# Routed expert blocks in plain fp32: weights loaded straight to their place, sixteen splits off GpSimd, expert numbers read a block ahead

## The chip, the cores and the metric

The kernel runs on one core of a Trainium2 chip. The metric is the device time of one execution in microseconds. One core has a matrix engine (TensorE), a vector engine (VectorE), an activation engine (ScalarE), a general engine (GpSimd) and a queue engine (SyncE) that here only issues transfers. In the rows they are called PE (PEld is its weight load), DVE, ACT, POOL and SP.

## The reference

Four layers follow one another, each added to its input: an attention over 1601 context rows, a feed-forward with 16 experts, a second attention over the same context, and a second feed-forward. x is 4 x 256 rows of 256 numbers in fp32. Only the last layer is touched:

```python
def _L1_ffn_ref(x, router_w, router_bias, Wu, Wg, Wd, Su, Sg, Sd):   # DIM 256, EXPERT_DIM 128, 16 experts, top 2
    logits = flat @ router_w.T
    scores = jax.nn.softmax(logits, axis=-1)
    _, topk_idx = jax.lax.top_k(logits + router_bias, TOPK)
    topk_scores = jnp.take_along_axis(scores, topk_idx, axis=-1)
    topk_scores = topk_scores / topk_scores.sum(-1, keepdims=True)
    combine = jnp.einsum('nk,nke->ne', topk_scores, jax.nn.one_hot(topk_idx, N_EXPERTS, dtype=scores.dtype))
    for e in range(N_EXPERTS):
        h = jax.nn.silu(flat @ Wu[e]) * (flat @ Wg[e])
        out = out + combine[:, e:e + 1] * (h @ Wd[e])
    for s in range(N_SHARED):                                        # one shared expert, 256 wide
        out = out + jax.nn.silu(flat @ Su[s]) * (flat @ Sg[s]) @ Sd[s]
```

## The kernel before

The program is written out by hand, one stream of instructions for each engine with semaphores between them. It has four stages: A (first attention, and the keys and values of the second), B (first feed-forward), C (second attention, up to about 679 us) and D (second feed-forward).

Products need nearly fp32 precision. Mostly they are made of three fast ones: each operand is split into a rounded part (the _hi or h tiles, fp32r) and the rest (_lo or l), and the helper mm3 (L582, its three matmuls are L584 to L586) issues hi x hi, hi x lo and lo x hi into the same PSUM bank. In the second attention, the product of probabilities and values (L837) is a single plain fp32 matmul instead.

Stage D before the blocks. SyncE waits for the last attention output (cx_rdy), issues seven small loads of constants (L493: router weights, a triangle, block numbers and so on) and then loads 18 weight tiles of 128x768 through four staging buffers e_raw (expert_tile, L488), each reuse waiting for d_w. Two tiles belong to the shared expert, sixteen to the routed ones. A tile holds gate and up weights in its first 512 columns and down weights in the last 256. GpSimd splits each tile into e_hi (a cast, L566) and e_lo (a subtraction, L568). Meanwhile TensorE makes the output projection, VectorE adds the residual and normalizes in products of 128x256 (L1559, L1564), takes statistics again (L1179, L1182), normalizes for this layer (L1187), splits the router's weights (L1572, L1574), and with TensorE and ScalarE transposes the result (xTh, xTl). The router's matmuls follow, the top two experts are chosen on VectorE (L1591 to L1618), which ends in pos_i, the row number of each token in a list sorted by expert. Each expert's rows are padded to blocks of 128: 31 blocks (NBLK) in all. GpSimd then scatters the tokens into x_slots in memory (16 indirect transfers, L573), while TensorE does the shared expert.

The block loop. For block j, SyncE loads 128 rows (slots_in, L501, four buffers); TensorE transposes them (slots_T, L943); ScalarE writes xbh (L1156), VectorE xbl (L1657); TensorE reads the block's expert number into a register (value_load, L947) and makes gate and up in one 256 column product for each half of the input width, that is six matmuls by mm3 (gate_up); ScalarE applies silu (L1160), VectorE multiplies (L1661); TensorE transposes the hidden block (hidden_T, L962); ScalarE and VectorE split it (hbh L1164, hbl L1665); TensorE makes the down product, three matmuls (expert_down); VectorE copies it to yb (L1671), and SyncE stores it (L510). TensorE runs the stages of four blocks interleaved: transposes of j+2, gate and up of j+1, hidden transpose of j, down of j-1. After all blocks GpSimd gathers two rows per token (L579) and VectorE mixes them (L1687, L1689).

Ahead of stage B SyncE also fills x_slots with zeros (L430) and then goes on with B's weight tiles (load_rest, L329).

Of the kernel before, what the change touches and what calls it, by code (L numbers as in the profile page):

```python
# [71 lines left out]
def build(nc, a, out, stop="D"):  # L72
# [8 lines left out]
    with ExitStack() as ctx:  # L81
# [95 lines left out]
        with ExitStack() as s:  # L177
# [3 lines left out]
            e_hi = Dt("e_hi", [P, NTILE, WC], F32R)  # L181
# [5 lines left out]
            xbh, xbl = Dt("xbh", [P, 2, KT * P], F32R), Dt("xbl", [P, 2, KT * P], F32R)  # L187
            sb_, hb = Dt("sb_", [P, 2, P]), Dt("hb", [P, 2, P])
            hbh, hbl = Dt("hbh", [P, 2, P], F32R), Dt("hbl", [P, 2, P], F32R)
# [3 lines left out]
            Dt("gap2", [P, 560])  # L193
            e_lo = Dt("e_lo", [P, NTILE, WC], F32R)
            e_raw = Dt("e_raw", [P, 4, WC])
# [63 lines left out]
        d_in = [sem(f"d_in{n}") for n in range(4)]  # L259
# [3 lines left out]
        xT_rdy, xb_hi, xb_lo, GU_rdy, sl_rdy, hm_rdy, hT_rdy, hb_hi, hb_lo, Y_rdy, y_ev = (  # L263
            sem(n) for n in ("xT_rdy", "xb_hi", "xb_lo", "GU_rdy", "sl_rdy", "hm_rdy", "hT_rdy", "hb_hi", "hb_lo", "Y_rdy", "y_ev"))
# [56 lines left out]
        def _(sp):  # L321
# [100 lines left out]
            for t, s in ((wq_raw[:], a["wqT"].rearrange("(k p) n -> p k n", p=P)), (bq[:], a["bq"]),  # L422
                         (wo_raw[:], a["woT"].rearrange("(k p) n -> p k n", p=P)),
                         (bo[:], a["bo"].rearrange("(o n) -> o n", o=1).broadcast_to([P, D])),
                         (gam[:], a["gam"].rearrange("(o n) -> o n", o=1).broadcast_to([P, D])),
                         (bet[:], a["bet"].rearrange("(o n) -> o n", o=1).broadcast_to([P, D])),
                         (rs[:], a["rs"].rearrange("(o n) -> o n", o=1).broadcast_to([P, 1]))):
                sp.dma_start(t, s).then_inc(cw_in, 16)
            for h in range(2):
                sp.dma_start(xs_d.rearrange("(j p) d -> p j d", p=P)[:, :, h * P:(h + 1) * P], zero[:].bitcast(F32).unsqueeze(1).broadcast_to([P, NBLK, P])).then_inc(x_zero, 16)  # L430
# [54 lines left out]
            def expert_tile(k):  # L485
# [4 lines left out]
            for t, s in ((gw_raw_d[:], a["gw1"].rearrange("(k p) n -> p k n", p=P)), (gb_d[:], a["gb1"].rearrange("(o n) -> o n", o=1).broadcast_to([P, E])),  # L490
                         (rev[:], a["rev"]), (tri_d[:], a["tri16"]), (steps[:], a["steps"]), (blk[:], a["blk"]),
                         (up_raw[:], a["upper"])):
                sp.dma_start(t, s).then_inc(d_cst, 16)  # L493
            for k in range(NTILE):
                expert_tile(k)
# [22 lines left out]
        def _(pool):  # L518
# [45 lines left out]
            for k in range(NTILE):  # L564
# [24 lines left out]
        def _(pe):  # L589
# [300 lines left out]
            def shared_hidden(n):  # L890
                k, half = n // 2, n % 2
                ct = SC0 + n
                s = slice(half * 512, half * 512 + 512)
                pe.wait_ge(d_w, k + 1)
                pe.wait_ge(silu_rdy, ct)
                for q in range(KT):
                    w = slice(q * 2 * P, q * 2 * P + P)
                    mm = mm3(pe, ps[:, 4, :], e_hi[:, k, w], e_lo[:, k, w], xTh[:, q, s], xTl[:, q, s], q == 0, q == 1)
                mm.then_inc(G_rdy, 1)
                pe.wait_ge(mul1_rdy, ct)  # L900
                for q in range(KT):
                    w = slice(q * 2 * P + P, (q + 1) * 2 * P)
                    mm = mm3(pe, ps[:, 5, :], e_hi[:, k, w], e_lo[:, k, w], xTh[:, q, s], xTl[:, q, s], q == 0, q == 1)
                mm.then_inc(U_rdy, 1)

            def shared_down(n):
                k, half = n // 2, n % 2
                pe.wait_ge(hl_rdy, SC0 + n + 1)
                for j in range(4):
                    t, s = 4 * half + j, slice(j * P, (j + 1) * P)  # L910
                    mm = mm3(pe, ps[:, t // 2, (t % 2) * D:(t % 2 + 1) * D], hh_d[:, half, s], hl_d[:, half, s],
                             e_hi[:, k, 2 * D:3 * D], e_lo[:, k, 2 * D:3 * D], False, False)
# [25 lines left out]
            def slots_T(j):  # L938
                pe.wait_ge(xb_in[j % XR], 16 * (j // XR + 1))
                if j >= 2:  # L940
                    pe.wait_ge(xb_lo, j - 1)
# [3 lines left out]

            def gate_up(j):
                expert[j] = pe.value_load(eb_i[0:1, j:j + 1], min_val=0, max_val=E - 1)  # L947
                pe.wait_ge(xb_lo, j + 1)
                if j >= 2:
                    pe.wait_ge(hm_rdy, j - 1)  # L950
                for k in range(KT):
                    w = slice(k * 2 * P, (k + 1) * 2 * P)
                    rh, rl = (t[:, NSH1:NTILE, w][:, bass.ds(expert[j], 1), :].rearrange("p o n -> p (o n)") for t in (e_hi, e_lo))
                    s = slice(k * P, (k + 1) * P)
                    mm = mm3(pe, ps[:, 2 + j % 2, 0:2 * P], xbh[:, j % 2, s], xbl[:, j % 2, s], rh, rl, k == 0, k == 1)
                mm.then_inc(GU_rdy, 1)

            def hidden_T(j):
                pe.wait_ge(hm_rdy, j + 1)
                if j >= 2:  # L960
                    pe.wait_ge(hb_lo, j - 1)
                pe.transpose(ps[:, 4 + j % 2, 0:P], hb[:, j % 2, :], ident[:]).then_inc(hT_rdy, 1)  # L962

            def expert_down(j):
                pe.wait_ge(hb_lo, j + 1)
                if j >= 2:
                    pe.wait_ge(y_ev, j - 1)
                rh, rl = (t[:, NSH1:NTILE, 2 * D:3 * D][:, bass.ds(expert[j], 1), :].rearrange("p o n -> p (o n)") for t in (e_hi, e_lo))
# [17 lines left out]
        def _(act):  # L986
# [167 lines left out]
            def slots_hi(j):  # L1154
                act.wait_ge(xT_rdy, j + 1)
                act.activation(xbh[:, j % 2, :], ps[:, j % 2, 0:KT * P], ACT.Copy).then_inc(xb_hi, 1)  # L1156
# [5 lines left out]
            def hidden_hi(j):  # L1162
                act.wait_ge(hT_rdy, j + 1)
                act.activation(hbh[:, j % 2, :], ps[:, 4 + j % 2, 0:P], ACT.Copy).then_inc(hb_hi, 1)  # L1164

            for j in range(-2, NBLK + 1):
                if j + 2 < NBLK:
                    slots_hi(j + 2)
                if 0 <= j + 1 < NBLK:
                    gate_silu(j + 1)  # L1170
                if 0 <= j < NBLK:
                    hidden_hi(j)
# [3 lines left out]
        def _(dve):  # L1176
# [478 lines left out]
            def slots_lo(j):  # L1655
                dve.wait_ge(xb_hi, j + 1)
                dve.tensor_tensor(xbl[:, j % 2, :], ps[:, j % 2, 0:KT * P], xbh[:, j % 2, :].bitcast(F32), ALU.subtract).then_inc(xb_lo, 1)  # L1657

# [3 lines left out]

            def hidden_lo(j):
                dve.wait_ge(hb_hi, j + 1)
                dve.tensor_tensor(hbl[:, j % 2, :], ps[:, 4 + j % 2, 0:P], hbh[:, j % 2, :].bitcast(F32), ALU.subtract).then_inc(hb_lo, 1)  # L1665
# [7 lines left out]
            for j in range(-2, NBLK + 1):  # L1673
                if j + 2 < NBLK:
                    slots_lo(j + 2)
                if 0 <= j + 1 < NBLK:
                    hidden_mul(j + 1)
                if 0 <= j < NBLK:
                    hidden_lo(j)
# [69 lines left out]
```

## Time and profile before

| | us |
|---|---|
| three runs | 871.08, 874.21, 874.29 |
| median | 874.21 |
| the profiled execution | 871.58 |
| its span in the profile | 869.7 |
| stage D in it, from 679 | 190.7 |
| of that, the block loop from its first transpose to the start of its last copy to yb | 64.4 |

Times in the rows are microseconds from the start of the span; durations of one instruction are in ns where the row says mean. A matmul's record includes the time in which the array fills and drains, so that records of one engine overlap; the distance of two starts is what one costs. The share of busy time is that of an engine over the span.

### The profile page before, as it was taken

To read this page: it belongs to the slowest core of one execution; us is meant where nothing else is said; L and a number is where in the kernel's file an instruction comes from. 1 tells how busy PE (TensorE), PEld (TensorE's weight loads), DVE (VectorE), ACT (ScalarE), POOL (GpSimd) and SP (SyncE) were. 2 spreads that over 40 slices of the span, in tenths; PEclk is the share of its full clock that TensorE was granted. 3 is DMA by queue.
4 is the path that set the end of the run, shared out by engine and by line. 5 is a ranking of instruction groups with operands and counts; after the bars stand their busy time and mean duration, and the time that the engine had idled before them with its cause. 6 is when DMAs were issued, how large, how long until landed. Compare 5 with 4: busy or idle time off the path is not lost.

```text
span 869.7 us, 14654 instructions
## 1 busy us (share of the span) xinstructions
PE 710.4 (82%) x5556; PEld 537.7 (62%) x5556; DVE 571.9 (66%) x1077; ACT 395.7 (45%) x555; POOL 156.6 (18%) x126
## 2 busy tenths in 40 slices
PE   4899998996789999999956999999999504858850
PEld 3778787984678888888843444444444302647740
DVE  7765656555866666666664777777777796546633
ACT  2524242433122222223226999999999201234420
POOL 6343434200000000000000000000000498330015
PEclk9999999997999999999986999999999855969995
DMA  6474746429333334333792999968840442134424
GB/s 216 159 226 145 227 158 214 177 85 306 98 90 108 119 92 126 96 115 105 140 161 51 195 147 122 194 89 145 140 61 2 129 136 73 37 107 130 135 85 127
DMA packets 63977, 114.52 MB, mean 132 GB/s; under 512 B 12064, under 2 KB 42272, under 8 KB 62896
## 3 DMA queue, kind: packets, MB, share of 16 engines
q1 hardware_dynamic: 61376, 108.30, 49.4%
q0 software_dynamic: 1536, 4.20, 1.5%
q10 hardware_dynamic: 1008, 1.25, 0.4%
q8 instruction: 38, 0.62, 0.4%
q14 instruction: 19, 0.16, 0.1%
HBM read 78.86 MB, written 31.70 MB: 127 GB/s over the span
## 4 chain that ended last, share of the span: by engine, by line
PE 42%; issue 16%; ACT 16%; POOL 9%; DVE 8%; DMA 6%; SPq 2%; POOLq 0%; ACTq 0%; DVEq 0%
ACT p L1130 13%; PE ps L584 12%; PE ps L585 11%; PE ps L586 11%; POOL e_lo L568 3%; PE ps L837 2%; DMA raw<-in_ctxT 2%; PE ps L819 2%; DMA raw<-in_ctxN 2%; POOL yg L579 2%; POOL cTl L557 2%; POOL e_hi L566 1%; POOL cNl L544 1%; DMA k_lo<-kl 1%; ACT cNh L1029 1%
## 5 line engine op out<-in xcount | busy, mean ns | idle before, releaser
L1130 ACT ACTIVATE p<-ps,kbias 128x1024 f32<-128x1024 f32 (+1 forms) x208 | 208.6, 1425 | 1.3 <-PE ps L819 1.3
L1509 DVE TENSOR_SCALAR p<-p 128x1024 f32<-128x1024 f32 (+1 forms) x208 | 144.1, 693 | 58.0 <-ACT p L1130 56.5
L837 PE MATMUL ps<-p,vsl 128*17 128x256 f32 (+1 forms) x1664 | 113.3, 387 | 0.7 <-DVE p L1509 0.7
L819 PE MATMUL ps<-qst,kst 48*128 48x256 f32 (+1 forms) x832 | 100.0, 329 | 14.4 <-DMA qst<-ql 5.9
L819 PEld LDWEIGHTS ps<-qst,kst 48*128 48x128 f32 (+1 forms) x832 | 61.2, 186 | 75.7 <-ACT p L1130 45.0
L1092 ACT ACTIVATE hh<-h 128x512 fp32r<-128x512 f32 x50 | 31.6, 632 | 138.7 <-DVE h L1441 114.8
L562 POOL MEMSET ones<- 128x128 f32 x1 | 0.2, 206 | 508.2 <-DMA up_raw<-in_upper 508.2
L584 PE MATMUL ps<-xTh,w_hi 128*128 128x512 f32 x200 | 80.0, 400 | 5.2 <-DVE h L1437 4.4
L585 PE MATMUL ps<-xTl,w_hi 128*128 128x512 f32 x200 | 79.3, 397 | 0.0
L586 PE MATMUL ps<-xTh,w_lo 128*128 128x512 f32 x200 | 79.2, 396 | 0.0
L837 PEld LDWEIGHTS ps<-p,vsl 128*17 128x17 f32 (+1 forms) x1664 | 37.7, 97 | 37.6 <-issue 3.9
L584 PE MATMUL ps<-w_hi,hh 128*128 128x256 f32 x200 | 57.7, 289 | 1.5 <-DVE hl L1443 1.5
L1443 DVE TENSOR_TENSOR hl<-h,hh 128x512 fp32r<-128x512 f32 x50 | 34.6, 692 | 36.6 <-ACT hh L1092 36.6
L1437 DVE TENSOR_TENSOR h<-silu,ps 128x512 f32<-128x512 f32 x50 | 34.4, 688 | 36.5 <-PE ps L586 22.6
L585 PE MATMUL ps<-w_lo,hh 128*128 128x256 f32 x200 | 57.4, 287 | 0.0
L586 PE MATMUL ps<-w_hi,hl 128*128 128x256 f32 x200 | 57.2, 286 | 0.0
L595 PE MATMUL ps<-ident,xn 128*128 128x128 f32 x48 | 11.8, 426 | 51.2 <-DVE xn L1187 51.2
L584 PEld LDWEIGHTS ps<-xTh,w_hi 128*128 128x128 f32 x200 | 38.0, 190 | 13.4 <-DVE h L1437 5.8
L544 POOL TENSOR_TENSOR cNl<-raw,cNh 128x1024 fp32r<-128x1024 f32 (+1 forms) x16 | 31.3, 1980 | 78.7 <-ACT cNh L1029 78.7
L586 PEld LDWEIGHTS ps<-xTh,w_lo 128*128 128x128 f32 x200 | 37.9, 189 | 9.0
L595 PEld LDWEIGHTS ps<-ident,xn 128*128 128x128 f32 x48 | 9.4, 222 | 53.0 <-DVE xn L1187 53.0
L585 PEld LDWEIGHTS ps<-xTl,w_hi 128*128 128x128 f32 x200 | 37.9, 189 | 6.6
(279 smaller groups left out, 1653.6 us busy)
## 6 DMA issues: line engine op xcount, KB each, us to landing
kst<-k_hi SPq DMA_DIRECT2D x64, 200.2 KB, 7.6
w_raw<-in_w SPq DMA_DIRECT2D x25, 384.0 KB, 3.0
v_one<-vst SPq DMA_DIRECT2D x4, 1768.0 KB, 9.2
vsl<-v_one SPq DMA_DIRECT2D x4, 1768.0 KB, 15.7
e_raw<-in_w SPq DMA_DIRECT2D x18, 384.0 KB, 3.0
kst<-k_lo SPq DMA_DIRECT2D x32, 200.2 KB, 8.4
raw<-in_ctxN SPq DMA_DIRECT2D x12, 512.0 KB, 6.0
k_hi<-kh SPq DMA_DIRECT2D x24, 256.0 KB, 2.6
```

What stands on the lines that cost most here:

```text
L544: pool.tensor_tensor(cNl[:, c0:c0 + w, :], src, cNh[:, c0:c0 + w, :].bitcast(F32), ALU.subtract).then_inc(ctx_split, 1)
L568: pool.tensor_tensor(e_lo[:, k, :], e_raw[:, k % 4, :], e_hi[:, k, :].bitcast(F32), ALU.subtract).then_inc(d_w, 1)
L584: e.matmul(o, lh, rh, start=first, stop=False, skip_group_check=True)
L585: e.matmul(o, lh, rl, start=False, stop=False, skip_group_check=True)
L586: return e.matmul(o, ll, rh, start=False, stop=last, skip_group_check=True)
L819: mm = pe.matmul(ps[0:rows, 2 * (x % RING) + t, c * SEQ:(c + 1) * SEQ], kst[r, job % KSL, c, m * P:m * P + rows], qst[r, b, 2 * g + c, :], ...
L837: mm = pe.matmul(ps[32 * j:32 * j + VW, 6 + job % 2, 0:SEQ], vsl[0:rows, b % 2, at_:at_ + VW], p32[0:rows, x % PBUF, (2 * t + c) * SEQ:(2 ...
L1092: act.activation(hh[:, half, :], h32[:, half, :], ACT.Copy).then_inc(hh_rdy, 1)
L1130: act.activation(p32[0:rows, x % PBUF, :], psf[0:rows, bank * 512:bank * 512 + 1024], ACT.Exp, scale=0.25, bias=kbias[0:rows, col:col + 1] ...
L1437: dve.tensor_tensor(h32[:, half, :], silu[:, half, :], ps[:, 5, :], ALU.mult).then_inc(mul1_rdy, 1)
L1443: dve.tensor_tensor(hl[:, half, :], h32[:, half, :], hh[:, half, :].bitcast(F32), ALU.subtract).then_inc(hl_rdy, 1)
L1509: dve.tensor_scalar(t, t, CLO, CHI, ALU.max, ALU.min).then_inc(p_clip, 1)
```

## The change

Five things change, all in stage D:

- The constants' seven loads are issued ahead of the zero fill of x_slots, before stage B, not after the attention.
- All 18 weight tiles are loaded unsplit into one tile e_w: two transfers of a tile for the shared expert, two of eight tiles each for the routed ones. No staging buffers are left, so no load waits for GpSimd.
- GpSimd splits only the two shared tiles, into sh_hi and sh_lo.
- In the block loop the operands aren't split: ScalarE writes xbT and hbT as plain fp32, VectorE's two subtractions are gone, and each mm3 becomes one plain fp32 matmul.
- The expert number of block j+2 is read after gate and up of block j+1 (expert_of), not directly before its use.

```diff
@@ SyncE, ahead of stage B
+            for t, s in ((gw_raw_d[:], ...), (gb_d[:], ...), (rev[:], a["rev"]), (tri_d[:], a["tri16"]), (steps[:], a["steps"]), (blk[:], a["blk"]), (up_raw[:], a["upper"])):
+                sp.dma_start(t, s).then_inc(d_cst, 16)
             for h in range(2):
                 sp.dma_start(xs_d..., zero...).then_inc(x_zero, 16)
             load_rest(FFN["B"])
@@ SyncE, after the attention (the same seven loads are gone from here)
             sp.wait_ge(cx_rdy, NJ)
-                if k >= 4:
-                    sp.wait_ge(d_w, k - 3)
-                sp.dma_start(e_raw[:, k % 4, :], a["w1"][k]).then_inc(d_in[k % 4], 16)
+            for k in range(NSH1):
+                sp.dma_start(e_w[:, k, :], a["w1"][k]).then_inc(d_in[0], 16)
+            for n in range(2):
+                sp.dma_start(e_w[:, NSH1 + 8 * n:NSH1 + 8 * n + 8, :], a["w1"][...].rearrange("k p c -> p k c")).then_inc(d_in[1], 16)
@@ GpSimd
-            for k in range(NTILE):
-                pool.wait_ge(d_in[k % 4], 16 * (k // 4 + 1))
-                pool.tensor_copy(e_hi[:, k, :], e_raw[:, k % 4, :]).then_inc(d_hi, 1)
+            for k in range(NSH1):
+                pool.wait_ge(d_in[0], 16 * NSH1)
+                pool.tensor_copy(sh_hi[:, k, :], e_w[:, k, :]).then_inc(d_hi, 1)
                 pool.wait_ge(d_hi, k + 1)
-                pool.tensor_tensor(e_lo[:, k, :], e_raw[:, k % 4, :], e_hi[:, k, :].bitcast(F32), ALU.subtract).then_inc(d_w, 1)
+                pool.tensor_tensor(sh_lo[:, k, :], e_w[:, k, :], sh_hi[:, k, :].bitcast(F32), ALU.subtract).then_inc(d_w, 1)
@@ TensorE, block loop
             def gate_up(j):
-                expert[j] = pe.value_load(eb_i[0:1, j:j + 1], min_val=0, max_val=E - 1)
-                pe.wait_ge(xb_lo, j + 1)
+                pe.wait_ge(xb_ev, j + 1)
...
-                    mm = mm3(pe, ps[:, 2 + j % 2, 0:2 * P], xbh[:, j % 2, s], xbl[:, j % 2, s], rh, rl, k == 0, k == 1)
+                    mm = pe.matmul(ps[:, 2 + j % 2, 0:2 * P], xbT[:, j % 2, k * P:(k + 1) * P], weights_of(j, slice(k * 2 * P, (k + 1) * 2 * P)),
+                                   start=k == 0, stop=k == KT - 1, skip_group_check=True)
...
             def expert_down(j):
-                mm3(pe, ps[:, 6 + j % 2, 0:D], hbh[:, j % 2, :], hbl[:, j % 2, :], rh, rl, True, True).then_inc(Y_rdy, 1)
+                pe.matmul(ps[:, 6 + j % 2, 0:D], hbT[:, j % 2, :], weights_of(j, slice(2 * D, 3 * D)),
+                          start=True, stop=True, skip_group_check=True).then_inc(Y_rdy, 1)
-            pe.wait_ge(d_w, NTILE)
+            pe.wait_ge(d_in[1], 32)
             pe.wait_ge(eb_rdy, 1)
+            expert_of(0)
...
                     gate_up(j + 1)
+                if 0 < j + 2 < NBLK:
+                    expert_of(j + 2)
                 if 0 <= j < NBLK:
                     hidden_T(j)
@@ VectorE, block loop: slots_lo and hidden_lo are gone; ScalarE's slots_hi and hidden_hi write xbT and hbT
```

TensorE, one round of the block loop before: transposes of a later block, the expert number's load, gate and up, the hidden transpose, down. An ISA or REGISTER_ALU row sets an address register.

```order
L943 MATMUL ps<-ident,xb 128x128 x2
L947 TENSOR_LOAD eb_i
L947 ISA x2
L584 ISA
L584 MATMUL ps<-e_hi,xbh 128x256
L585 REGISTER_ALU
L585 MATMUL ps<-e_lo,xbh 128x256
L586 MATMUL ps<-e_hi,xbl 128x256
...
L962 MATMUL ps<-ident,hb 128x128
L584 ISA
L584 MATMUL ps<-e_hi,hbh 128x256
```

The same round of the changed program:

```order
L940 MATMUL ps<-ident,xb 128x128 x2
L954 ISA
L954 MATMUL ps<-e_w,xbT 128x256
L954 ISA
L954 MATMUL ps<-e_w,xbT 128x256
L944 TENSOR_LOAD eb_i
L944 ISA x2
L962 MATMUL ps<-ident,hb 128x128
L968 ISA
L968 MATMUL ps<-e_w,hbT 128x256
```

Twelve matmul instructions became six, and the load moved from ahead of gate and up to behind them.

SyncE between the attention's last key load and the first blocks, before:

```order
DMA kst<-k_hi 16x2x1602
DMA gw_raw_d<-in_gw 128x2x16
DMA gb_d<-in_gb 128x16
DMA rev<-in_rev 128x16
DMA tri_d<-in_tri 128x256
DMA steps<-in_steps 128x8
DMA blk<-in_blk 128x31
DMA up_raw<-in_upper 128x128
DMA e_raw<-in_w 128x768 x18
DMA xb<-x_slots 128x256 x8
```

And in the changed program:

```order
DMA kst<-k_hi 16x2x1602
DMA e_w<-in_w 128x768 x2
DMA e_w<-in_w 128x8x768 x2
DMA xb<-x_slots 128x256 x8
```

The seven small loads now stand ahead of the zero fill, and the eighteen tile loads became four transfers.

## Rows read from the trace of the kernel before

**Rows 1.** The page, part 1: busy time, share of the span, instructions.

```profile
PE 710.4 (82%) x5556; PEld 537.7 (62%) x5556; DVE 571.9 (66%) x1077; ACT 395.7 (45%) x555; POOL 156.6 (18%) x126
```

**Rows 2.** Stretches: length, busy PE, PEld, DVE, ACT, POOL, then clock, DMA share, GB/s.

```profile
690.00:700.00 10.00, 0.00 (x0) 0.00 (x0) 9.93 (x17) 0.30 (x1) 9.76 (x8) 0.52 0.48 151
...
770.00:780.00 10.00, 3.99 (x17) 3.31 (x18) 3.82 (x8) 2.71 (x5) 1.73 (x2) 0.50 0.39 118
...
800.00:820.00 20.00, 16.63 (x122) 14.27 (x121) 12.14 (x40) 8.23 (x31) 0.00 (x0) 1.00 0.44 132
```

**Rows 3.** Timeline (start, us, engine, line), VectorE beside GpSimd; the chain's transfer.

```profile
682.36 3.53 DMA e_raw<-in_w
...
691.47 11.52 DVE L1559 SCALAR_TENSOR_TENSOR xn<-xn,mv,gam 128x256 f32<-128x256 f32 x8
692.15 1.86 POOL L568 TENSOR_TENSOR e_lo<-e_raw,e_hi 128x768 fp32r<-128x768 f32 x1
...
695.05 1.86 POOL L568 TENSOR_TENSOR e_lo<-e_raw,e_hi 128x768 fp32r<-128x768 f32 x1
```

**Rows 4.** Timeline, VectorE from the residual to the router's first matmul.

```profile
703.14 11.45 DVE L1564 SCALAR_TENSOR_TENSOR resid<-xn,rstd,resid 128x256 f32<-128x256 f32 x8
714.62 2.71 DVE L1179 BATCH_NORM_STATS2 st<-resid 128x6 f32<-128x256 f32 x8
...
718.62 10.31 DVE L1187 TENSOR_SCALAR xn<-resid,mv,rstd 128x256 f32<-128x256 f32 x8
...
729.06 1.68 DVE L1574 TENSOR_TENSOR gwl_d<-gw_raw_d,gwh_d 128x32 fp32r<-128x32 f32 x1
...
733.19 0.61 PE L584 MATMUL ps<-xTh,gwh_d 128*16 128x512 f32 x1 [3.08 <-DVE xTl L1193]
```

**Rows 5.** Timeline, the same shapes elsewhere: final mix, and ahead of stage C.

```profile
442.21 2.71 DVE L1179 BATCH_NORM_STATS2 st<-resid 128x6 f32<-128x256 f32 x8
...
452.09 0.50 PE L584 MATMUL ps<-xTh,wqh 128*128 128x512 f32 x1 [1.41 <-DVE xTl L1193]
...
850.15 0.48 DVE L1689 SCALAR_TENSOR_TENSOR resid<-yg,m_w,resid 128x256 f32<-128x256 f32 x1
850.55 0.48 DVE L1687 SCALAR_TENSOR_TENSOR resid<-yg,m_w,resid 128x256 f32<-128x256 f32 x1
```

**Rows 6.** Timeline: row numbers, first transposes and last output of the blocks.

```profile
750.17 0.17 DVE L1618 CAST pos_i<-pos_f 128x16 int32<-128x16 f32 x1
...
775.57 1.26 PE L943 MATMUL ps<-ident,xb 128*128 128x128 f32 x4 [9.05 <-DMA xb<-x_slots]
...
839.97 0.42 DVE L1671 COPY yb<-ps 128x256 f32<-128x256 f32 x1 [0.40 <-PE ps L586]
```

**Rows 7.** Timeline of one block in the middle of the loop.

```profile
808.02 0.38 PE L943 MATMUL ps<-ident,xb 128*128 128x128 f32 x2
...
808.70 0.38 PE L584 MATMUL ps<-e_hi,xbh 128*128 x1 [0.29 <-DVE hb L1661]
...
809.98 0.38 PE L943 MATMUL ps<-ident,xb 128*128 128x128 f32 x2
810.01 0.29 DVE L1661 TENSOR_TENSOR hb<-sb_,ps 128x128 f32<-128x128 f32 x1 [0.73 <-ACT sb_ L1160]
```

**Rows 8.** Stage B's weight tiles: issue and split (timeline), landing of three (line L329).

```profile
212.92 18.84 SPq L329 DMA_DIRECT2D w_raw<-in_w  x3
...
229.81 0.55 DVE L1365 CAST w_hi<-w_raw 128x768 fp32r<-128x768 f32 x1
...
DMA to landing us min/median/max: 3.0/5.4/10.8
```

**Rows 9.** Groups by form (count, busy us, mean ns), plain and split; timeline of plain ones.

```profile
L837 PE MATMUL ps<-p,vsl 128*17 128x256 f32 x1536 | 106.1, 387 | 0.4 <-DVE p L1509 0.4
...
L586 PE MATMUL ps<-e_hi,hbl 128*128 x31 | 8.7, 281 | 0.0
...
661.42 1.06 PE L837 MATMUL ps<-p,vsl 128*17 128x256 f32 x16
```

More of the change, by code:

```diff
@@ L192, in build @@
             logit_d = Dt("logit_d", [E, NT * P])
-            Dt("gap2", [P, 560])
-            e_lo = Dt("e_lo", [P, NTILE, WC], F32R)
-            e_raw = Dt("e_raw", [P, 4, WC])
+            Dt("gap2", [P, 3 * D + 560 + 256])
+            sh_hi, sh_lo = Dt("sh_hi", [P, NSH1, WC], F32R), Dt("sh_lo", [P, NSH1, WC], F32R)
+            Dt("gap3", [P, 13500])
             gw_raw_d = Dt("gw_raw_d", [P, KT, E])
@@ L258, in build @@
         x_zero, d_cst, tri_rdy = sem("x_zero"), sem("d_cst"), sem("tri_rdy")
-        d_in = [sem(f"d_in{n}") for n in range(4)]
+        d_in = [sem(f"d_in{n}") for n in range(2)]
         d_hi, d_w = sem("d_hi"), sem("d_w")
@@ L262, in build @@
         slots_out, xb_in = sem("slots_out"), [sem(f"xb_in{n}") for n in range(XR)]
-        xT_rdy, xb_hi, xb_lo, GU_rdy, sl_rdy, hm_rdy, hT_rdy, hb_hi, hb_lo, Y_rdy, y_ev = (
-            sem(n) for n in ("xT_rdy", "xb_hi", "xb_lo", "GU_rdy", "sl_rdy", "hm_rdy", "hT_rdy", "hb_hi", "hb_lo", "Y_rdy", "y_ev"))
+        xT_rdy, xb_ev, GU_rdy, sl_rdy, hm_rdy, hT_rdy, hb_ev, Y_rdy, y_ev = (
+            sem(n) for n in ("xT_rdy", "xb_ev", "GU_rdy", "sl_rdy", "hm_rdy", "hT_rdy", "hb_ev", "Y_rdy", "y_ev"))
         y_out = [sem(f"y_out{n}") for n in range(4)]
@@ L428, in _ @@
                 sp.dma_start(t, s).then_inc(cw_in, 16)
+            for t, s in ((gw_raw_d[:], a["gw1"].rearrange("(k p) n -> p k n", p=P)), (gb_d[:], a["gb1"].rearrange("(o n) -> o n", o=1).broadcast_to([P, E])),
+                         (rev[:], a["rev"]), (tri_d[:], a["tri16"]), (steps[:], a["steps"]), (blk[:], a["blk"]),
+                         (up_raw[:], a["upper"])):
+                sp.dma_start(t, s).then_inc(d_cst, 16)
             for h in range(2):
@@ L484, in _ @@
             sp.wait_ge(cx_rdy, NJ)
-            def expert_tile(k):
-                if k >= 4:
-                    sp.wait_ge(d_w, k - 3)
-                sp.dma_start(e_raw[:, k % 4, :], a["w1"][k]).then_inc(d_in[k % 4], 16)
[L490 to L493, printed above, removed]
-            for k in range(NTILE):
-                expert_tile(k)
+            for k in range(NSH1):
+                sp.dma_start(e_w[:, k, :], a["w1"][k]).then_inc(d_in[0], 16)
+            for n in range(2):
+                sp.dma_start(e_w[:, NSH1 + 8 * n:NSH1 + 8 * n + 8, :], a["w1"][NSH1 + 8 * n:NSH1 + 8 * n + 8].rearrange("k p c -> p k c")).then_inc(d_in[1], 16)
             sp.wait_ge(slots_out, 16 * 2 * NT)
@@ L940, in slots_T @@
                 if j >= 2:
-                    pe.wait_ge(xb_lo, j - 1)
+                    pe.wait_ge(xb_ev, j - 1)
                 for k in range(KT):
@@ L944, in slots_T, with expert_of, weights_of @@
                 mm.then_inc(xT_rdy, 1)
+            def expert_of(j):
+                expert[j] = pe.value_load(eb_i[0:1, j:j + 1], min_val=0, max_val=E - 1)
+            def weights_of(j, w):
+                return e_w[:, NSH1:NTILE, w][:, bass.ds(expert[j], 1), :].rearrange("p o n -> p (o n)")
             def gate_up(j):
-                expert[j] = pe.value_load(eb_i[0:1, j:j + 1], min_val=0, max_val=E - 1)
-                pe.wait_ge(xb_lo, j + 1)
+                pe.wait_ge(xb_ev, j + 1)
                 if j >= 2:
@@ L960, in hidden_T @@
                 if j >= 2:
-                    pe.wait_ge(hb_lo, j - 1)
+                    pe.wait_ge(hb_ev, j - 1)
                 pe.transpose(ps[:, 4 + j % 2, 0:P], hb[:, j % 2, :], ident[:]).then_inc(hT_rdy, 1)
             def expert_down(j):
-                pe.wait_ge(hb_lo, j + 1)
+                pe.wait_ge(hb_ev, j + 1)
                 if j >= 2:
                     pe.wait_ge(y_ev, j - 1)
-                rh, rl = (t[:, NSH1:NTILE, 2 * D:3 * D][:, bass.ds(expert[j], 1), :].rearrange("p o n -> p (o n)") for t in (e_hi, e_lo))
-                mm3(pe, ps[:, 6 + j % 2, 0:D], hbh[:, j % 2, :], hbl[:, j % 2, :], rh, rl, True, True).then_inc(Y_rdy, 1)
-            pe.wait_ge(d_w, NTILE)
+                pe.matmul(ps[:, 6 + j % 2, 0:D], hbT[:, j % 2, :], weights_of(j, slice(2 * D, 3 * D)),
+                          start=True, stop=True, skip_group_check=True).then_inc(Y_rdy, 1)
+            pe.wait_ge(d_in[1], 32)
             pe.wait_ge(eb_rdy, 1)
+            expert_of(0)
             pe.wait_ge(add_rdy, 8)
@@ L1171, in _ @@
                 if 0 <= j < NBLK:
-                    hidden_hi(j)
+                    hidden_ev(j)
         @block.vector
```

36 lines of the change are left out of this document (11 added, 25 removed).

## The prediction

> **What bounds the kernel now.** I read the page first [rows 1]: TensorE is busy for 82% of the 869.7 us span, so one might look there. But the change touches only what follows the second attention, from about 679 us on, so I next read the busy time by stretch [rows 2]. Between 690 and 700 us TensorE does nothing at all while VectorE and GpSimd are both busy for nearly the whole stretch; between 800 and 820 us TensorE leads with 16.6 of 20 us. So the last 190 us have two different limits.
>
> The first is a string of VectorE work: the residual, its statistics, a normalization, its transposes and the routing. GpSimd splits 18 weight tiles beside it. In [rows 3] eight VectorE products of 128x256 from two SBUF operands take 11.52 us, 1.44 each, and they keep step with GpSimd: a subtraction of 1.86 us and a cast follow each other there with a period of 2.90 us, in which two VectorE operations end. [Rows 4] show the rest of the string: eight more such products 11.45 us, then eight statistics at 0.34 each, eight normalizations 10.31 us, and a subtraction of merely 128x32 elements that takes 1.68 us. [Rows 5] are the same shapes with no GpSimd arithmetic beside them: products at the kernel's end last 0.48 and start 0.40 apart, and the normalization before the query projection needs 9.88 us from its first statistics (442.21) to the first matmul behind it (452.09), against 18.57 here (714.62 to 733.19). What the slow operations have in common is that they read two SBUF operands or are a one-input operation with scalars on SBUF alone; the statistics, with one input, are no slower beside GpSimd (2.71 us for eight in both places). So VectorE waits for GpSimd here, operation by operation.
>
> The Trainium skill, SBUF — State Buffer, in its part on port contention, says that a VectorE instruction with two SBUF inputs, or in a two-port mode, and a GpSimd instruction that reads SBUF lock each other out for whole instructions, and that one-input work isn't touched. The trace agrees (1.44 against 0.40 us, and 0.34 unchanged).
>
> The second limit: row numbers are ready at 750.34, GpSimd scatters the rows from then on, the first block is transposed at 775.57 and the last output leaves PSUM from 839.97 to 840.39 [rows 6]. In the loop a block costs 1.96 us [rows 7]: two transposes start at 808.02, gate and up at 808.70, the next transposes at 809.98. The last 1.28 us hold ten products, 0.128 each; the first 0.68 hold two, so 0.42 us is bare. The expert number is loaded just there.
>
> **The change part by part.**
>
> Sixteen weight splits leave GpSimd; two stay. The two remaining tiles are now first in the queue, issued at about 679.0 instead of 682.4, because the constants moved away. A tile landed 3.5 us after its issue in the old place [rows 3], and two cast-subtract pairs at 2.9 us end near 689, before the first long VectorE product at 691.47. What runs on VectorE until then is statistics or reads PSUM. So the string runs uncovered: 16 products at 0.40 instead of 1.43, from 691.47 to 714.62: the two groups took 11.44 and 11.48 us to the next start and will take 3.2 to 3.3 each, which saves 16.3. The normalization with its small split falls to the 9.88 us of its twin, which saves 8.7. Sum 25.0 us. Next in line are routing on VectorE, then the scatter, neither shortened: they simply start 25 us earlier. TensorE in the twin is as cold at its start as here, so no clock gain is booked. Bounds: 20 if GpSimd's two tiles land late and reach into the first eight products, 26 at most.
>
> The weights now arrive in four transfers straight to their place, 7.1 MB. Before, they were paced by GpSimd at 2.7 to 2.9 us a tile with the DMA engines at 0.48 [rows 2], 151 GB/s. Even at that pace they are there at 679 + 47 = 726 us; the block loop wants them at 775.6 - 25 = 750.6. Cost nothing; cover 24 us; at under 99 GB/s it would be gone and every us of lateness counts.
>
> The seven constant loads go ahead of the zero fill and the first feed-forward's third weight tile in the SyncE queue: seven issues at 0.45, 3.2 us. The tile is issued at 212.92 and lands at the latest 10.8 us on, at 223.7; VectorE splits it at 229.81, not waiting for it [rows 8]. Cover 6.1 us, so nothing; without it, 3.2. The loads are small, and no engine waits for them until 680.
>
> In the block loop six of twelve TensorE products disappear: nine products of split operands become three plain ones, three transposes stay. Each plain product is one instruction but leaves two records. Where does the trace show one? The attention's value products are plain fp32 of 256 columns: 387 ns per record against 281 for a split product of the same columns [rows 9]. The difference, 0.10 us, over the split's pitch of about 0.12 makes 0.22 per record, 0.44 per product. The upper bound is their pitch: 16 records in 1.06 us, with four column groups side by side, is 0.265 per record, 0.53 per product. The lower bound is the split pitch for each record, 0.24. I take 0.44, since the pitch also holds waits for the neighbours. A block is then 3 x 0.128 + 3 x 0.44 = 1.71 us of array time.
>
> By the Trainium skill, Perfetto Trace Analysis, on engine utilization, the array gives half its output rate in the fp32 low-high form; at 2.4 GHz that would be 0.213 us for 256 columns, and a block of 1.66 by it.
>
> The expert number's load is moved behind gate and up of the block before. What lies ahead of it is 0.88 us of array work instead of 0.26. Issue before was 12 x 0.128 plus 0.42 = 1.96, all of the block; now it is 6 x 0.128 + 0.42 = 1.19, under 1.71, so the sequencer gets ahead and the load is hidden. That it can get ahead while the array is slow I read from the cold start of the loop (clock 0.50 in the stretch 770 to 780). If it can't, the load costs its 0.42 a block.
>
> VectorE loses two of its four operations a block and ScalarE keeps its three. Neither binds: before, with all of them, they were busy 12.1 and 8.2 of 20 us [rows 2]. The chain gate and up, silu, multiplication, hidden transpose: the array leaves gate and up at 808.70 + 6 x 0.128 = 809.47, and the multiplication ends at 810.30 [rows 7], 0.83 later. The transpose's turn comes only 0.13 + 0.44 + 0.26 + 0.88 = 1.71 us later. No new wait.
>
> From 775.57 to the start of the last copy at 839.97 the loop took 64.4 us = 31 x 1.96 + 3.6. I keep the 3.6 for filling and draining, and add 1.0 because its first 7 us run at the half clock, where plain products cost most: 31 x 1.71 + 4.6 = 57.6. That saves 6.8 us. Ends: 1.19 a block (sequencer alone) saves 23; 0.53 a product with an uncovered load (0.38 + 1.59 + 0.42 = 2.39) costs 14.
>
> The gather and final mix behind it keep their length.
>
> **Sum.** Against the profiled execution's own 871.58 us: 871.6 - 25.0 - 6.8 = 839.8. The shown runs are 871.08, 874.21 and 874.29, so the profiled one lies 2.6 under the median; half of that added gives 841.
>
> **The rivals.**
>
> (a) The load stays uncovered or plain products take 0.53: blocks of 2.0 to 2.25 us, 1 to 9 over before, so 871.6 - 25 + 1 to 9 = 848 to 856. For it: with a full-speed clock the trace never shows the sequencer ahead in this loop. Against: the sums above. Chance 0.20.
>
> (b) The plain products are as quick per record as split ones, the sequencer binds at 1.2 to 1.5 a block: 31 x 0.46 to 0.76 saved, less the 1.0: 824 to 833. For it: column groups side by side may stretch the records I read. Chance 0.08.
>
> (c) GpSimd isn't what slows VectorE, and only the loop gains: 871.6 - 6.8 = 865. Against: the twins in rows 5. Chance 0.02.
>
> (d) The weights land late: a new wait at the loop's head eats part of the 25, 845 to 865. Against: 24 us of cover. Chance 0.04.
>
> (e) Slower than before: TensorE stays at its lower level, 1.2 of 2.4 GHz, through the block loop. It is there when the loop starts, after 9 us of idling. Plain products then take 0.88 and transposes 0.26, a block 3.4 us; 31 x (3.4 - 1.96) - 25 = +20, 891. It outweighs the gain from blocks of 2.77 us on. Against: before, the clock was 1.00 from 800 to 820 with TensorE busy 16.6 of 20 us, and plain products ran all through the attention. Chance 0.03.
>
> **How the numbers follow.** Forecast 841, blocks of 1.6 to 1.85 with the 25 intact, chance 0.63. The range 832 to 856 takes in all of it and (a), and leaves out most of (b), (c), (e) and part of (d), under 0.2. A measurement here can tell about 0.5%, 4.4 us, from no change. All but (e) are faster than that: faster 0.96, same 0.01, slower 0.03.
>
> **What would show it.** In the changed profile: VectorE's sixteen products at a pitch of 0.40 and 9.9 us from the first statistics to the router's matmul; row numbers at about 725; first block transposed near 750.6; block pitch 1.71 with TensorE unbroken, no bare time behind the transposes; each plain product two records of about 0.22 pitch. A pitch over 1.9 with idle before the hidden transpose means (a); clock 0.5 in the loop means (e); TensorE waiting for the weights' transfer means (d). The prediction is wrong above all if the plain product's price is misread, since each 0.1 us on it is 9 us.

## The result

| | before | changed |
|---|---|---|
| median, us | 872.64 (4 runs, 868.16 to 874.29) | 835.83 (4 runs, 832.85 to 836.82) |
| ratio | | 0.958, 95% interval 0.953 to 0.963 |
| profiled execution | 871.58, span 869.7 | 832.85, span 831.0 |

Run again later beside two experiments, the changed kernel gave 834.71 (5 runs, 832.54 to 838.52), ratio 0.958 (0.954 to 0.961). The forecast was 841, the range 832 to 856.

**The changed kernel's profile.** First the string of VectorE work. Timeline from the first statistics to the router's first matmul, the columns as in [rows 3]:

```profile
686.65 2.71 DVE L1555 BATCH_NORM_STATS2 st<-xn 128x6 f32<-128x256 f32 x8
...
690.07 3.26 DVE L1562 SCALAR_TENSOR_TENSOR xn<-xn,mv,gam 128x256 f32<-128x256 f32 x8
...
693.47 3.26 DVE L1567 SCALAR_TENSOR_TENSOR resid<-xn,rstd,resid 128x256 f32<-128x256 f32 x8
696.76 2.71 DVE L1182 BATCH_NORM_STATS2 st<-resid 128x6 f32<-128x256 f32 x8
...
700.76 2.67 DVE L1190 TENSOR_SCALAR xn<-resid,mv,rstd 128x256 f32<-128x256 f32 x8
...
703.55 0.19 DVE L1577 TENSOR_TENSOR gwl_d<-gw_raw_d,gwh_d 128x32 fp32r<-128x32 f32 x1
...
706.38 0.40 PE L581 MATMUL ps<-xTh,gwh_d 128*16 128x512 f32 x1 [1.56 <-DVE xTl L1196]
```

These are the shapes of [rows 3, 4]. Eight products take 3.26 us where they took 11.52, eight normalizations 2.67 instead of 10.31, the small subtraction 0.19 instead of 1.68. The statistics, 2.71, are what they were. From the first product to the router's matmul it is 706.38 - 690.07 = 16.31 us, against 733.19 - 691.47 = 41.72 before: 25.4 us less.

The stretches, columns as in [rows 2]. The third is the cold head of the block loop, the fourth its middle:

```profile
690.00:700.00 10.00, 0.00 (x0) 0.00 (x0) 9.86 (x33) 0.30 (x1) 0.00 (x0) 0.53 0.59 229
...
700.00:710.00 10.00, 6.89 (x36) 5.11 (x37) 5.80 (x18) 3.21 (x6) 0.00 (x0) 0.79 0.00 1
...
745.00:750.00 5.00, 3.15 (x9) 2.17 (x10) 0.00 (x0) 2.05 (x3) 0.00 (x0) 0.50 0.53 157
...
760.00:770.00 10.00, 10.00 (x56) 8.40 (x56) 3.97 (x13) 5.22 (x20) 0.00 (x0) 1.00 0.54 164
```

From 690 to 700 VectorE ends 33 operations where it ended 17, and GpSimd is idle. The weights move at 229 GB/s and in the next stretch next to nothing moves (1 GB/s): they are all there by 700, some 47 us before the block loop. In the loop TensorE is busy 10.00 us of 10.

One block in the middle, and the last copy to yb, timeline:

```profile
779.77 0.38 PE L940 MATMUL ps<-ident,xb 128*128 128x128 f32 x2
779.99 1.03 PE L954 MATMUL ps<-e_w,xbT 128*128 x4
780.86 0.27 PE L962 MATMUL ps<-ident,hb 128*128 128x128 f32 x1
780.97 0.60 PE L968 MATMUL ps<-e_w,hbT 128*128 x2
781.40 0.38 PE L940 MATMUL ps<-ident,xb 128*128 128x128 f32 x2
...
800.91 0.42 DVE L1666 COPY yb<-ps 128x256 f32<-128x256 f32 x1 [0.16 <-PE ps L968]
```

A block is 781.40 - 779.77 = 1.63 us where it was 1.96 [rows 7]. Its parts follow without a gap: two transposes 0.22, gate and up 0.87 for two plain products (four records), the hidden transpose 0.11, down 0.43. From the first transposes (746.70) to the last copy the loop takes 54.2 us, against 64.4.

### The profile page after: what moved, and what is told of

It reads as the page before. It is cut to its first block, busy times and chain, and to the rows that moved or that the text cites. A ratio compares the mean times of both kernels' runs of the same rounds, so it can differ in the third digit from the quotient of the medians.

```text
span 831.0 us, 14267 instructions
## 1 busy us (share of the span) xinstructions
PE 706.3 (85%) x5463; PEld 534.8 (64%) x5463; DVE 529.2 (64%) x1015; ACT 396.2 (48%) x555; POOL 114.0 (14%) x94
## 3 DMA queue, kind: packets, MB, share of 16 engines
q10 hardware_dynamic: 1008, 1.25, 0.4%
## 4 chain that ended last, share of the span: by engine, by line
PE 51%; ACT 17%; issue 11%; DVE 11%; POOL 5%; DMA 4%; SPq 1%; POOLq 0%; ACTq 0%; DVEq 0%
ACT p L1133 13%; PE ps L581 13%; PE ps L582 12%; PE ps L583 12%; PE ps L954 3%; PE ps L834 2%; POOL x_slots L570 2%; PE ps L816 2%; POOL yg L576 2%; PE ps L968 2%; DMA raw<-in_ctxT 1%; PE ps L592 1%; DMA raw<-in_ctxN 1%; DVE st L1182 1%; ACT cNh L1032 1%
## 5 line engine op out<-in xcount | busy, mean ns | idle before, releaser
L581 PEld LDWEIGHTS ps<-w_hi,hh 128*128 128x128 f32 x200 | 38.5, 193 | 4.4 <-DVE hl L1446 2.1
L582 PEld LDWEIGHTS ps<-w_lo,hh 128*128 128x128 f32 x200 | 38.5, 193 | 2.1
```

Of the source, the lines that this page charges most:

```text
L581: e.matmul(o, lh, rh, start=first, stop=False, skip_group_check=True)
L582: e.matmul(o, lh, rl, start=False, stop=False, skip_group_check=True)
```

## The experiments

The clock level of a TensorE stretch is read from the durations too: a split product's record of 512 columns is 0.40 us at the upper level and 0.61 at the lower. Where a time is that of a single execution, what is concluded rests on its trace and not on that time.

### GpSimd splits put back

```diff
+            for k in range(NEX1):     # 16 times, from the shared tiles to scratch
+                pool.tensor_copy(scr_hi[:], e_w[:, k % NSH1, :]).then_inc(d_hi, 1)
+                pool.wait_ge(d_hi, NSH1 + k + 1)
+                pool.tensor_tensor(scr_lo[:], e_w[:, k % NSH1, :], scr_hi[:].bitcast(F32), ALU.subtract).then_inc(d_hi2, 1)
```

> The changed kernel with sixteen more cast-and-subtract pairs of 128x768 on GpSimd behind the two shared tiles, read from the shared tiles and written to a scratch tile that nobody reads. The transfers, the block loop and everything else stay as changed. Theory (GpSimd's arithmetic holds VectorE up, operation by operation): the pairs run at 2.7 to 2.9 us from 686 to about 731 us, the sixteen products of 128x256 on VectorE go back to about 1.43 us each and the normalization to 1.3, so the string from the first of these products to the router's first matmul takes 41 us again instead of 16.3, the loop stays at 1.63 a block, and the time is 835.8 + 25 = 861, ratio to the kernel before about 0.987. Rival (the tile transfers or the waits for them slowed VectorE, not the arithmetic): 836, string 16.3 us.

862.65 us (5 runs, 859.34 to 864.91), ratio 0.989 (0.985 to 0.993) to before. Against the changed kernel's 835.83 it is 27 us slower. Timeline of VectorE in it:

```profile
689.80 11.51 DVE L1568 SCALAR_TENSOR_TENSOR xn<-xn,mv,gam 128x256 f32<-128x256 f32 x8
...
712.95 2.71 DVE L1188 BATCH_NORM_STATS2 st<-resid 128x6 f32<-128x256 f32 x8
...
716.94 9.77 DVE L1196 TENSOR_SCALAR xn<-resid,mv,rstd 128x256 f32<-128x256 f32 x8
```

The durations of before are back, with nothing on TensorE or in the transfers changed: from the first product to the router's first matmul it is 730.96 - 689.80 = 41.2 us again, and the block loop stays at 54.0. The splits on GpSimd, not the transfers or the staging buffers, held VectorE up. The kernel before, run beside it, took 872.39; the 9.7 us between the two are about what the block loop gained.

### GpSimd busy without reading

```diff
+            for k in range(3 * NEX1):
+                pool.memset(scr_hi[:].bitcast(F32), 0.0).then_inc(d_hi2, 1)
```

> The changed kernel with 48 GpSimd fills of 128x768 (write only, nobody reads them) in the place of the sixteen pairs. Theory by which only a GpSimd operation that reads holds up two-operand work: the sixteen products keep their pitch of 0.40, while the one-input normalization with scalars (0.33 each in the changed kernel) is held up to 0.7 or more, so the string grows by 3 to 6 us and the time by the same. Rival (any GpSimd work holds VectorE up): the products go to 0.7 or more each too, the string grows by 10 us or more. Second rival (a fill holds nothing up): 836 as in the changed kernel.

838.79 us, one execution. GpSimd is busy from 685.11 to 723.49 in it, and the string splits in two kinds. Timeline:

```profile
689.21 3.26 DVE L1566 SCALAR_TENSOR_TENSOR xn<-xn,mv,gam 128x256 f32<-128x256 f32 x8
...
699.89 6.19 DVE L1194 TENSOR_SCALAR xn<-resid,mv,rstd 128x256 f32<-128x256 f32 x8
706.01 0.79 DVE L1579 CAST gwh_d<-gw_raw_d 128x32 fp32r<-128x32 f32 x1
706.83 0.19 DVE L1581 TENSOR_TENSOR gwl_d<-gw_raw_d,gwh_d 128x32 fp32r<-128x32 f32 x1
```

The products and the subtraction, with two SBUF operands, don't wait for a GpSimd that only writes (3.26 and 0.19, as without it). The normalization with its one input does (6.19 against 2.67), and so does the cast (0.79 against 0.18). That is 3.5 + 0.6 us; the string is 4.0 us longer. The Trainium skill, SBUF — State Buffer, on who interferes with whom, describes both: an operation with two SBUF inputs meets a GpSimd operation that reads, not one that only writes, while a copy, cast or tensor_scalar in a two-port mode meets either. This trace agrees, with 0.40 us a product beside the fills and 1.44 beside the splits, and 0.77 us a normalization beside the fills. Beside the splits the same cast took 0.17: it started at 726.63, where GpSimd had ended a cast at 726.56 and began its subtraction at 726.65.

### The early load alone, in the kernel before

```diff
             def gate_up(j):
-                expert[j] = pe.value_load(eb_i[0:1, j:j + 1], min_val=0, max_val=E - 1)
...
                     gate_up(j + 1)
+                if 0 < j + 2 < NBLK:
+                    expert_of(j + 2)
```

> The kernel before with one edit: the expert number of block j+2 is read behind gate and up of block j+1, as in the changed kernel; all products stay split. Theory (in that loop issue binds: twelve matmul instructions at 0.128 and the load's 0.42 one after another, and the queue never runs ahead): the pitch stays 1.96 a block, time the same as before within 2 us. Rival (the load's latency is hidden as soon as six matmuls stand ahead of it): 1.54 a block, 31 x 0.42 = 13 us faster, ratio 0.985.

869.21 us (10 runs, 867.48 to 872.06), ratio 0.997 (0.995 to 0.999). A block of it, TensorE's timeline:

```profile
782.38 0.38 PE L943 MATMUL ps<-ident,xb 128*128 128x128 f32 x2
782.52 0.36 PE L584 MATMUL ps<-e_hi,xbh 128*128 x1
...
783.20 0.28 PE L586 MATMUL ps<-e_hi,xbl 128*128 x1
783.55 0.30 PE L964 MATMUL ps<-ident,hb 128*128 128x128 f32 x1
...
784.12 0.38 PE L943 MATMUL ps<-ident,xb 128*128 128x128 f32 x2
...
787.16 0.30 PE L964 MATMUL ps<-ident,hb 128*128 128x128 f32 x1
787.55 0.38 PE L584 MATMUL ps<-e_hi,hbh 128*128 x1
```

The bare time is no longer ahead of gate and up. It has moved with the load to behind them (783.20 to 783.55 where 0.12 is the pitch, 0.23 bare instead of 0.42). This block takes 1.74 us, but it is one of the short ones: the last 23 distances from one pair of transposes to the next are 1.83 to 2.02 us, 1.90 on average, against 1.89 to 2.25 and 2.00 in the kernel before. In the longer ones more time stands bare behind the hidden transpose (787.16 to 787.55); what sets that part wasn't tried. The loop is 61.1 us instead of 64.4. Moving the load is worth 3 us with split products, which is small, but the interval leaves out 1. It is neither the 0 of the theory nor the 13 of the rival: most of the load's time still shows.

### The load back ahead of gate and up, in the changed kernel

```diff
             def gate_up(j):
+                expert_of(j)
...
-                if 0 < j + 2 < NBLK:
-                    expert_of(j + 2)
```

> The changed kernel with the expert number's load back directly ahead of gate and up. Theory (six long plain products let the queue run ahead, issue needs 1.2 us of the 1.63): pitch 1.63 to 1.70, time within 2 us of 835.8. Rival (it was the new place that hid the load): the 0.42 is bare again, 2.0 a block, 13 us more, 849.

838.31 us (4 runs, 835.25 to 838.93), ratio 0.961 (0.957 to 0.965), beside 0.958. The loop is 54.0 us and unbroken:

```profile
782.38 0.38 PE L940 MATMUL ps<-ident,xb 128*128 128x128 f32 x2
782.60 1.03 PE L955 MATMUL ps<-e_w,xbT 128*128 x4
...
784.01 0.38 PE L940 MATMUL ps<-ident,xb 128*128 128x128 f32 x2
```

The pitch is 1.63 in either place. With plain products the load's place is indifferent in the loop; the two intervals of the whole time overlap.

### Down product twice

```diff
+                pe.matmul(ps[:, 6 + j % 2, 0:D], hbT[:, j % 2, :], weights_of(j, slice(2 * D, 3 * D)), start=True, stop=True, skip_group_check=True)
                 pe.matmul(ps[:, 6 + j % 2, 0:D], hbT[:, j % 2, :], weights_of(j, slice(2 * D, 3 * D)), start=True, stop=True, skip_group_check=True).then_inc(Y_rdy, 1)
```

> The changed kernel with the down product of every block issued twice (same operands, same result). Measures one plain product. Theory (the array binds, 0.43 a product): pitch 1.63 + 0.43 = 2.06 us a block, 31 x 0.43 = 13 us more. Rival (a chain over ScalarE and VectorE or issue binds, and a product of room is left): less than 5 us more.

846.24 us, one execution. Timeline:

```profile
767.41 0.38 PE L940 MATMUL ps<-ident,xb 128*128 128x128 f32 x2
...
768.61 0.60 PE L968 MATMUL ps<-e_w,hbT 128*128 x2
769.04 0.59 PE L970 MATMUL ps<-e_w,hbT 128*128 x2
769.47 0.38 PE L940 MATMUL ps<-ident,xb 128*128 128x128 f32 x2
```

The pitch is 2.06, so a plain product of 256 columns costs 0.43 us and all of it is on the path: the array sets the block. The loop took 67.1 us, 12.9 more.

### Single fp32r products, and then no load

```diff
-            e_w = Dt("e_w", [P, NTILE, WC])
+            e_w = Dt("e_w", [P, NTILE, WC], F32R)     # xbT and hbT likewise
```

> The changed kernel with the block loop's three products as single fast ones (fp32r operands, without the rest parts), so the low-order parts are left out of the routed experts' result. Nothing else differs. Theory (then issue binds: six matmuls at 0.12 and the load's 0.42): 1.15 to 1.3 us a block, 10 to 15 us less than the changed kernel in the loop, and time behind the load becomes bare again. Rival (the chain gate and up, silu, multiplication, transpose, or the transfers bind first): 1.4 or more a block.

828.76 us, one execution. The pitch fell only to 1.5 to 1.6, not to 1.15 to 1.3. The chain that ended last, three pieces and the next:

```profile
782.30 0.22 PE ps L940 x2
782.52 0.35 PE ps L954 x2
782.86 0.39 issue
783.26 0.30 PE ps L962
```

In each block about 0.4 us (0.39 to 0.44) stand under issue, just behind gate and up, where the load is. To tell the load from the chain over silu, it was left out:

```diff
-                expert[j] = pe.value_load(eb_i[0:1, j:j + 1], min_val=0, max_val=E - 1)
+                expert[j] = expert[0] if j else pe.value_load(eb_i[0:1, j:j + 1], min_val=0, max_val=E - 1)
```

> The run with single fp32r products in the block loop, with the expert number read once, for block 0, and used for all blocks: both the low-order parts and the choice of expert are left out. In the run with the load, a block took 1.57 us of which 0.40 stood bare in front of the hidden transpose, where the load of the number is. Theory: that bare time is the register load, and the array's own work is 1.17; a block takes 1.17 to 1.25 us, 31 x 0.35 = 11 us less than the 828.8, 817 to 819. Rival: it is the chain gate and up, silu, multiplication, hidden transpose that leaves TensorE waiting there, and the pitch stays at 1.45 to 1.57, 826 to 829.

819.32 us, one execution, 9.4 less. From the first copy to yb to the last it takes 31.1 us instead of 43.4, 1.04 a block instead of 1.45. (The whole kernel gained less because its row numbers came 2.3 us later in this execution.) The load, with the two ISA rows that go with it, was the bare time; the run doesn't tell these apart. What is left there is no single limit: waits for the rows and for VectorE alternate:

```profile
761.10 0.44 PE L940 MATMUL ps<-ident,xb 128*128 128x128 f32 x2 [0.45 <-DVE hb L1660]
...
762.60 0.44 PE L940 MATMUL ps<-ident,xb 128*128 128x128 f32 x2 [0.59 <-DMA xb<-x_slots]
```

Together: the load takes some 0.4 us of TensorE's sequencer, and whether that shows depended on the array work per instruction around it. It showed beside split and single products, which start 0.12 to 0.22 us apart, and it didn't beside plain ones of 0.43. That the sequencer gets ahead of the array there is the reading that fits these four runs; none measures its lead.

### The constants back behind the attention

```diff
             sp.wait_ge(cx_rdy, NJ)
+            for t, s in ((gw_raw_d[:], ...), ..., (up_raw[:], a["upper"])):
+                sp.dma_start(t, s).then_inc(d_cst, 16)
```

> The changed kernel with the seven loads of constants back behind the attention, ahead of the weight tiles. Theory: the shared tiles arrive 3.3 us later, GpSimd's two pairs end near 689.5 and touch the first product on VectorE at most by one operation, 0 to 2 us more. Rival (the early place cost something ahead of the first feed-forward, which comes back): 1 to 3 us less.

836.82 us (4 runs, 836.04 to 837.78), ratio 0.961 (0.958 to 0.963). The seven issues take 3.3 us (678.48 to 681.80), GpSimd waits 2.8 us for the shared tiles behind them, and its second subtraction now ends at 691.81 instead of 686.18. It still overlaps none of the long products (from 692.10, 3.25 for eight), by 0.3 us. VectorE waits for none of it, and the two intervals overlap: the move brought nothing that these runs resolve.

### Warming the clock before the loop

```diff
             shared_down(2 * NSH1 - 1)
+            for n in range(60):       # 84 and 100 in the next two
+                pe.matmul(ps[:, 6, 0:P], zero[:], zero[:], start=True, stop=True, skip_group_check=True)
```

> The changed kernel with 60 matmuls of 128x128 zeros behind the shared expert's last down product, about 7 us of work where TensorE waits for the scattered rows. Theory: the granted clock is at the upper level when the loop starts, the first blocks no longer run at the lower one, and the loop is 2 to 3 us shorter: 833. Rival (the clock falls all the same, or the filler delays the first transposes): the same or up to 2 us more.

837.11 us (6 runs, 835.24 to 841.07), ratio 0.962 (0.959 to 0.965): no gain. The 60 ended at 747.1, the rows came at 749.55, and the first four records of gate and up took 2.07 us, the lower level. The granted clock was 1.00 up to 748, 0.83 from 748 to 750 and 0.50 from 750 on. So the gap was closed:

> The changed kernel with 84 zero matmuls of 128 columns on TensorE behind the shared expert, where it else idles 7.9 us until the first rows are loaded. They run 0.1135 us each (60 took 6.81 us), so they reach up to some 0.1 us of the first transposes, where 60 left 2.45 us of idle and the clock had fallen again to its lower level. Theory: the idle time itself costs the clock; with no idle left the loop's first three rounds run at the upper level (2.07, 1.91 and 1.1 us of four records become 1.03 each), 2 to 2.5 us less from the first transposes to the last copy (54.2 to about 52), so the time falls to 833.5 against 835.8. Rival: the clock falls whatever TensorE does there, because it is granted by something other than this idle time; loop 54.2 to 54.8, time as the changed kernel or a little over.

> As the run with 84 zero matmuls, with 100 of them: 11.35 us, which reaches 1 to 2 us past the moment at which the first rows are there. Theory: loop warm from its start (about 52 us from first transposes to last copy), but the transposes start up to 1.9 us late, so the time is that of the changed kernel within 1 us, 834.5 to 836. Rival (clock not held by the fill): 837.5 to 838.

842.92 us (5 runs, 836.99 to 848.14) and 850.47 (5 runs, 841.26 to 852.58): both slower than without, which neither theory nor rival had. TensorE's timeline with 84, and the stretches with 84 and with 100:

```profile
736.36 3.24 PE L933 MATMUL ps<-zero 128*128 128x128 f32 x28
740.72 0.34 PE L933 MATMUL ps<-zero 128*128 128x128 f32 x2 [1.13 <-issue]
741.42 0.27 PE L933 MATMUL ps<-zero 128*128 128x128 f32 x1 [0.36 <-issue]
742.83 0.70 PE L933 MATMUL ps<-zero 128*128 128x128 f32 x3 [1.14 <-issue]
```

```profile
744.50:754.50 10.00, 10.00 (x49) 10.00 (x49) 0.19 (x1) 0.00 (x0) 0.00 (x0) 0.50 0.18 52
```

```profile
755.00:760.00 5.00, 5.00 (x25) 5.00 (x25) 0.00 (x0) 0.00 (x0) 0.00 (x0) 0.50 0.01 3
760.00:765.00 5.00, 5.00 (x25) 5.00 (x25) 0.00 (x0) 0.00 (x0) 0.00 (x0) 0.50 0.00 0
```

Two things happened. The fill was broken by idle times of 0.4 to 1.2 us which the trace puts under issue, and between them the clock fell (with 84 it was 1.00 from 740 to 741 and 0.50 from 742 to 743) to its lower level, where a zero product takes 0.21 us instead of 0.11. And it stayed there through more than 10 us in which TensorE was busy all the time, to rise only in the loop's real products (with 84, the first four records took 2.07 us, the next four 1.06). The fill so ran until 754.8 and 765.2. The first transposes came 34.5 and 38.3 us after the row numbers, where it was 25.6 in the changed kernel: 9 and 13 us late. The Trainium skill, TensorE: Matmul & The Clock Gate, on what actually happens, says that activity releases the throttle. By that the fill should have lifted the clock; these rows differ, and they decide. Whether it matters that the operands are zero is open: no run had others, and the 60 zero products ran at 1.00 to their end. What broke the fill is open as well.

> The changed kernel itself once more, beside the two runs with zero matmuls. Both theories: 832.9 to 836.8 as before. If the router's matmuls run at either clock level by chance (14.7 or 16.7 us from the router's first matmul to the row numbers in the traces so far), its runs lie in two groups some 2 us apart, and the level seen in this trace may be the other.

834.71 us, told above. Its five times, 832.5 to 838.5, form no two groups; that part of the expectation wasn't borne out.

## Why the prediction was right, and where its sum was off

The two profiled executions differ by 869.7 - 831.0 = 38.7 us of span, and the sum had 31.8. By its terms:

| term | predicted | measured |
|---|---|---|
| VectorE's string | -25.0 | -25.4 |
| router's first matmul to row numbers | 0 | -2.2 |
| row numbers to first transposes | 0 | +0.2 |
| block loop | -6.8 | -10.2 |
| gather and mix | 0 | +0.4 |
| end of the attention, same code | 0 | -2.6 |
| output projection and statistics, same code | 0 | +1.2 |

**The string: right in mechanism and size.** Products at 0.41, 9.62 us from the first statistics to the router's matmul where the twin in [rows 5] had promised 9.88. The splits put back show the cause. The fills show two kinds that the prediction had put together: two-operand work was held up only by a GpSimd that reads, the one-input normalization also by one that only writes.

**Weights, constants: right, free.** GpSimd was through with its two tiles at 686.2, ahead of the first product; the weights had 47 us of cover instead of the 24 that were counted on at the old pace. The third tile ahead of the first feed-forward was issued at 212.86, where it had been 212.92: the zero fill ahead of it took 5.63 us of the queue instead of 8.45, which made up for most of the seven issues.

**The plain product: right.** 0.43 against 0.44, measured by doubling one. That the group of plain records had to be read by duration and not by its pitch of 0.53 was the choice that mattered. No row ahead of the result showed that a difference in duration is one in pitch; the doubled product bears it out. The other estimate, a block of 1.66 from 0.213 us for 256 columns, doesn't follow: 0.213 a product would make 3 x 0.128 + 3 x 0.213 = 1.02, and 1.66 takes 0.213 for each of a product's two records. Measured it is 0.216 a record, 0.43 a product.

**The block loop: the term mis-sized.** Its working was 3 x 0.128 + 3 x 0.44 = 1.71 a block, plus 4.6. The transposes cost 0.11, not 0.128: that figure was the mean of ten instructions of which nine were split products. Block 1.63: 31 x 0.08 = 2.6 us. The 4.6 for filling, draining and the cold head were 54.2 - 31 x 1.627 = 3.8. Together the 3.4 us missed.

**The load: the result right, for a reason that is now narrower.** It is hidden as forecast, but not because it was moved, as the prediction had it (0.88 us of array work ahead of it instead of 0.26): with plain products it is hidden in the old place too, and with split ones most of it shows in the new place.

**The clock: not booked, and not the change's.** Between the router's matmul and the row numbers the changed kernel took 14.7 us at the upper clock in this trace. In the twelve traces of the changed kernel and its variants, the router's first matmul took 0.40 or 0.41 us in five (14.7 us to the row numbers) and 0.61 in seven (16.4 to 16.7); before it was 0.61 (17.0). The same code took either, so the 2.2 us are at least in part the luck of this trace. In the three traces with the long string (before, the early load alone, the splits put back) it was 0.61 each time, after a longer idle time of TensorE; three traces don't tell whether that is luck too. The +1.2 at the output projection goes with the clock in the same way, turned round. Its sixteen transposes, before, changed, and in the kernel before with the early load alone:

```profile
679.06 1.97 PE L863 MATMUL ps<-ident,cx 128*128 128x128 f32 x16 [0.82 <-DVE cx L1527]
```

```profile
676.48 3.25 PE L860 MATMUL ps<-ident,cx 128*128 128x128 f32 x16 [0.82 <-DVE cx L1530]
```

```profile
678.04 3.35 PE L863 MATMUL ps<-ident,cx 128*128 128x128 f32 x16 [0.82 <-DVE cx L1532]
```

Of fourteen traces only that of the kernel before had the upper clock there, in the others the sixteen took 2.92 to 3.48 us; the third row has its code and not its luck. The -2.6 ahead of it is spread too: these transposes started between 675.47 and 680.02 in the fourteen traces.

Leaving aside the router's clock and what lies ahead of the string, it is -25.4 - 10.2 + 0.6 = -35.0 us. The medians differ by 36.8; the runs don't divide the other 1.8. The forecast of 841 lies 5 us over the median: 3.4 of it is the mis-sized loop, the rest lies within what executions of one kernel differ by.

**The rivals.** (a) fell: blocks of 1.63, no bare time. (b) fell for the plain product, which takes 0.43. (c) fell by the splits put back. (d) fell: the transfer was over at 700. (e) was real for the first 5 us of the loop only: the clock was 0.50 up to 752 and 0.99 from 752 to 754.

## What to carry to other kernels

Before moving elementwise work to GpSimd because it is idle, look at which VectorE operations run beside it and compare them with the same shape elsewhere in the trace: here sixteen splits of 2.9 us on an idle engine cost 27 us on the busy one. Three split products took 0.36 us of array time and a plain one 0.43, and yet the loop with plain ones was the shorter: count instructions and loads per block beside the array's time before choosing. A plain product could be priced here by how much longer its records are than those of a neighbour with a known pitch.

## What the runs showed that was not expected

- The early load alone took 3.3 us off the split loop, where none or 13 had been expected.
- Single products stayed at 1.5 to 1.6 us a block where 1.15 to 1.3 had been expected, and without the load they took 1.04 where 1.17 to 1.25 had.
- TensorE kept its lower clock through more than 10 us of unbroken zero products.
- Sixty filler matmuls ran without a break; 84 and 100 were broken several times by up to 1.2 us, and their medians lie 8 and 16 us over that of the changed kernel run beside them.
- The clock level at the router's matmuls differed between executions with the same idle time ahead of them, worth 2 us.
